# A LoRA, attention and FFN-adapter kernel: x is loaded and split at other places of a step, and the output projection runs one batch ahead of the conditioned weights

## The reference

```python
h = x @ W.T + b + 2.0 * ((x @ A[id]) @ Bm[id])      # LoRA projection, an adapter per batch
q, k, v = h @ w_q, h @ w_k, h @ w_v
o = softmax(q @ k.T / sqrt(32)) @ v                 # 32 heads, 8 key/value heads
x = x + o @ w_o
y = x @ cond2[id2].T                                # a 1024x1024 weight per batch
gates = softmax over the 2 largest of 4 of (y @ router_w.T)
x = x + 4.0 * sum_e gates_e * (y @ A_e.T) @ B_e.T   # rank 16, 4 experts
```

## Time and profile before

| what | us |
|---|---|
| median of 3 runs | 1071.86 (1070.69 to 1072.41) |
| profiled execution, its own time | 1075.97 |
| its span | 1074.3 |
| PE busy, of the span | 1018.2 (95%) |
| DVE busy | 635.1 (59%) |
| ACT busy | 450.3 (42%) |
| POOL busy | 233.7 (22%) |

### The profile page before, as it was taken

The page is one execution under the profiler, slowest core; times in us unless marked ns, Lnnn a source line. Parts: engine busy times, 40 slices in busy tenths (PEclk is TensorE's granted clock), DMA queues, the critical chain, the costliest instruction groups (busy, mean ns, idle before and its releaser), DMA issues.

```text
span 1074.3 us, 17421 instructions
## 1 busy us (share of the span) xinstructions
PE 1018.2 (95%) x6934; PEld 822.1 (77%) x6934; DVE 635.1 (59%) x1071; ACT 450.3 (42%) x782; POOL 233.7 (22%) x224
## 2 busy tenths in 40 slices
PE   7999999999899998999989999899799999999997
PEld 6878787877578775777767787577488898898896
DVE  6562734567755578654776557664555655655653
ACT  5121223355544466543664556544523323323320
POOL 1000001133223333223331236443200100100100
PEclk9999999999899998999998999899989999999998
DMA  7030312011421124211132125435757667667531
GB/s 257 0 99 18 111 55 72 22 36 37 116 57 37 35 53 115 58 34 31 45 97 71 44 81 153 115 115 175 225 165 233 210 189 230 213 184 231 196 118 40
DMA packets 49888, 117.41 MB, mean 109 GB/s; under 512 B 7298, under 2 KB 26114, under 8 KB 45712
## 3 DMA queue, kind: packets, MB, share of 16 engines
q1 hardware_dynamic: 40080, 81.70, 26.0%
q0 software_dynamic: 9728, 34.61, 10.1%
HBM read 86.38 MB, written 18.89 MB: 98 GB/s over the span
## 4 chain that ended last, share of the span: by engine, by line
PE 83%; DVE 6%; ACT 4%; DMA 4%; POOL 1%; SPq 1%; issue 1%; ACTq 0%
PE psP L752 17%; PE psW L1038 16%; PE psF L254 11%; PE psG L1066 8%; PE psO L820 5%; PE psT L807 4%; PE psS L796 4%; PE psP L767 3%; PE psX L1281 3%; PE psO L824 3%; DVE q_stack L652 2%; PE psY L1300 2%; ACT probs L599 2%; ACT q_stack L565 1%; PE psF L265 1%; PE psM L831 1%
## 5 line engine op out<-in xcount | busy, mean ns | idle before, releaser
L672 DVE TENSOR_REDUCE nmax<-psS 128x2 f32<-128x512 f32 x256 | 164.7, 685 | 178.5 <-PE psS L796 176.8
L549 POOL TENSOR_TENSOR p_sum<-probs 128x512 f32<-128x512 f32 x128 | 167.1, 1305 | 395.3 <-ACT probs L599 395.1
L752 PE MATMUL psP<-x_hl,wq 128*128 128x512 f32 x960 | 238.1, 393 | 3.7 <-DVE q_stack L652 3.7
L752 PEld LDWEIGHTS psP<-x_hl,wq 128*128 128x128 f32 x960 | 174.8, 189 | 35.7 <-issue 4.4
L1038 PE MATMUL psW<-wq 128*128 128x256 f32 x1536 | 197.4, 284 | 1.6 <-DVE q_stack L652 1.1
L1038 PEld LDWEIGHTS psW<-wq 128*128 128x128 f32 x1536 | 191.1, 191 | 6.3 <-issue 1.5
L599 ACT ACTIVATE probs<-psT 128x512 f32<-128x512 f32 x256 | 139.1, 595 | 46.9 <-PE psT L807 45.8
L1047 ACT ACTIVATE cond_hi<-cond_raw 128x1024 fp32r<-128x1024 f32 x64 | 66.8, 1057 | 154.3 <-PE psG L1066 149.9
L1051 DVE TENSOR_TENSOR cond_lo<-cond_raw,cond_hi 128x1024 fp32r<-128x1024 f32 x64 | 78.3, 1235 | 89.7 <-ACT cond_hi L1047 89.6
L614 ACT ACTIVATE nmax_rows<-psM 16x128 f32<-16x128 f32 x64 | 17.1, 268 | 190.5 <-PE psM L831 190.5
L652 DVE TENSOR_TENSOR q_stack<-psP,q_stack 32x512 fp32r<-32x512 f32 x128 | 87.8, 686 | 8.0 <-ACT q_stack L565 5.9
(11 more groups left out here) (122 smaller groups left out, 1261.8 us busy)
## 6 DMA issues: line engine op xcount, KB each, us to landing
cond_raw<-in_cond POOLq DMA_DIRECT2D x64, 512.0 KB, 4.0
x_raw<-in_xT SPq DMA_DIRECT2D x32, 256.0 KB, 4.0
q_stack<-q_stack SPq DMA_DIRECT2D x32, 256.0 KB, 3.1
o_scratch<-o_sb SPq DMA_DIRECT2D x64, 128.0 KB
o_raw<-rden_scratch SPq DMA_DIRECT2D x32, 256.0 KB, 5.3
o_raw<-o_scratch SPq DMA_DIRECT2D x8, 1024.0 KB, 9.4
x_sb<-in_xT SPq DMA_DIRECT2D x8, 1024.0 KB, 6.8
outT<-x_sb SPq DMA_DIRECT2D x32, 256.0 KB, 2.5
```

What stands on the lines that cost most here:

```text
L549: pool.tensor_tensor(p_sum[:, heads], probs[:, 0, heads], probs[:, 1, heads], ALU.add).then_inc(sum_done, 1)
L672: dve.tensor_reduce(nmax[:, n % 2, 2 * hp:2 * hp + 2, qt], psS[:, i % 2].rearrange("p (h k) -> p h k", h=2), AX.X, ALU.max, negate=True).t ...
L752: mm = pe.matmul(out, wq[:, i, w, k * P:(k + 1) * P], x[:, k, part], start=(k == 0 and n_ == 0), stop=False)
```

## The change

It does four things. (1) `WORK` is laid out anew: each q and k unit is split among other half steps; q1 lies wholly in the step before its pair, v0 in part 0 of s = 0 and v1 in part 1 of s = 1; (9, 1), (11, 1) and (12, 1) are empty; `project_u` is cut in two halves of four k-tiles. (2) The loads of x stand at the head of SP's steps 11 (k-tiles 0 to 5) and 12 (6, 7), where they stood at the end of 10, 11 and 12. ACT's hi parts are 0 to 5 in step 11, 6 and 7 in step 12. DVE's lo parts are 0 to 2 ahead of maxima 2 and 3 of step 12, 3 to 5 behind them, 6 and 7 in step 13; q7 is copied out behind them. (3) The output projection runs a batch ahead: batch 1's tiles 0 to 4 stand in steps 16 to 18 and its last three in `first()`; batch n then does the projection of n+1. x has three slots. The o and x of batch 1 are loaded at the end of step 12, o of batch 2 at step 17. (4) The last two batches share the last 8 tiles (`two()`), at which 16 rows are placed.

```diff
 WORK = [
...
-    (["q5:5-8"], ["q6:0-2"]),
-    (["q6:2-4"], ["q6:4-6"]),
+    (["q5:5-8"], ["q6:0-3"]),
+    (["q6:3-6"], []),
     (["q6:6-8"], ["q7:0-3"]),
-    (["q7:3-5"], ["q7:5-6"]),
+    (["q7:3-6"], []),
     (["q7:6-8"], []),
-    (["+u"], ["+k0:0-5"]),
-    (["+k0:5-8", "+q0:0-2"], ["+q0:2-8"]),
-    (["+q1:0-2"], ["+q1:2-4"]),
+    (["+u:0-4"], ["+u:4-8"]),
+    (["+k0"], ["+q0"]),
+    (["+q1:0-4"], ["+q1:4-8"]),
 ]
...
 def evacuated(n, part):
...
+    behind_x = [(p, u) for p, u in finished(n, 0) if u == "q7" and p + 1 < PAIRS]
+    if part:
+        return finished(n, 1) + behind_x
...
         def step(n):
+            if more:
+                for k in {11: range(0, 6), 12: range(6, KT)}.get(s, ()):
+                    load_x(sp, p + 1, k)
             if 1 <= n <= N:
...
-            if more:
-                for k in {10: range(0, 3), 11: range(3, 6), 12: range(6, KT)}.get(s, ()):
-                    load_x(sp, p + 1, k)
...
-                for k in {11: range(0, 3), 12: range(3, KT)}.get(s, ()):
+                for k in {11: range(0, 6), 12: range(6, KT)}.get(s, ()):
                     split_x_hi(act, p + 1, k)
...
+            if more:
+                for k in {12: range(0, 3), 13: range(6, KT)}.get(s, ()):
+                    split_x_lo(dve, p + 1, k)
...
+            if more and s == 12:
+                for k in range(3, 6):
+                    split_x_lo(dve, p + 1, k)
...
-    FIRST_TILES = {(12 + (m + 1) // 2, (m + 1) % 2): m for m in range(KT)}
+    TWO_AT = [[0, 1], [2, 3], [4, 5], [6, 7], [], [8, 9, 10], [11, 12, 13, 14, 15], []]
+    TWO_SPLIT = [[2, 3], [4, 5], [6, 7], [], [8, 9], [10, 11, 12], [13, 14, 15], []]
+    AHEAD = 5
+    FIRST_TILES = {(12 + (m + 1) // 2, (m + 1) % 2): divmod(m, KT) for m in range(KT + AHEAD)}
...
         if s == 12:
             sp.wait_ge(before.proj_done, PAIRS * NS)
+            load_o(sp, 1)
+            load_x(sp, 1)
             sp.dma_start(ra_raw[:], RA).then_inc(const_landed, 16)
-        if s == 13:
-            load_x(sp, 1)
-            load_o(sp, 1)
+        if s == 17:
+            load_o(sp, 2)
...
-        if part == 1 and s == 9:
-            normalise(dve, 0)
-        if part == 1 and s == 11:
-            scale_lo(dve, 0)
-        m = FIRST_TILES.get((s, 0) if part else (s - 1, 1))
-        if m is not None:
-            residual(dve, 0, m)
+        if part == 1 and s in (9, 13):
+            normalise(dve, (s - 9) // 4)
+        if part == 1 and s in (11, 15):
+            scale_lo(dve, (s - 11) // 4)
+        tile = FIRST_TILES.get((s, 0) if part else (s - 1, 1))
+        if tile is not None:
+            residual(dve, *tile)
...
+        def two():
+            n = B - 2
+            for m in range(KT):
+                w_o_tile(pe, n + 1, m, range(4))
+                if m == 4:
+                    turn_g(n)
+                if m == 7:
+                    y_tile(n + 1, 2)
+                    y_tile(n + 1, 3)
+                    turn_g(n + 1)
+                w_o_tile(pe, n + 1, m, range(4, KT))
+                if m == 4:
+                    middle(n)
+                for r in TWO_AT[m]:
+                    cond_row(pe, n + r // KT, r % KT)
+                if m == 1:
+                    turn_gated(n)
+                if m in (2, 3):
+                    y_tile(n, 2 * (m - 2))
+                    y_tile(n, 2 * (m - 2) + 1)
+                if m == 6:
+                    turn_gated(n + 1)
+                    y_tile(n + 1, 0)
+                    y_tile(n + 1, 1)
+            middle(n + 1)
```

More of the change, by code:

```diff
@@ L308, in work @@
 def work(n, part):
-    for w in FIRST.get(n, WORK[n % STEPS])[part] if n < N else []:
+    for w in WORK[n % STEPS][part] if n < N else []:
         p = n // STEPS + (w[0] == "+")
@@ L323, in evacuated @@
 def evacuated(n, part):
[L325 to L328, removed]
+    behind_x = [(p, u) for p, u in finished(n, 0) if u == "q7" and p + 1 < PAIRS]
+    if part:
+        return finished(n, 1) + behind_x
+    late = [(p, u) for p, u in finished(n - 1, 0) if u == "v0"] if n else []
+    return late + [(p, u) for p, u in finished(n, 0) if u != "v0" and (p, u) not in behind_x]
 def unit(p, u):
@@ L723, in free, with project_u @@
                 pe.wait_ge(before.tile_lo, CHUNKS * KT)
-        def project_u(p):
-            free(p, "u")
-            pe.wait_ge(a_lo_done, p + 1)
+        def project_u(p, first, end):
+            if first == 0:
+                free(p, "u")
+                pe.wait_ge(a_lo_done, p + 1)
             out = psP[0:64, bank(p, "u")]
-            for k in range(KT):
+            for k in range(first, end):
                 pe.wait_ge(x_lo_done, KT * p + k + 1)
@@ L772, in run_work @@
             for p, u, first, end in work(n, part):
-                if n == 0 and u == "q1":
-                    continue
                 if u == "u":
-                    project_u(p)
+                    project_u(p, first, end)
                 elif u[0] == "v":
@@ L908, in finish_stage @@
     const_landed, fb_landed = sem("const_landed"), sem("fb_landed")
[L909 removed]
+    o_landed, x_landed = ([sem(f"{v}_landed_{c}") for c in range(slots)] for v, slots in (("o", 2), ("x", 3)))
     o_normal, o_hi_done, o_lo_done = sem("o_normal"), sem("o_hi_done"), sem("o_lo_done")
@@ L1110, in ahead_tensor @@
     def ahead_tensor(pe, n, part):
-        m = FIRST_TILES.get((n - LAST, part))
-        if m is not None:
-            w_o_tile(pe, 0, m, range(KT))
+        tile = FIRST_TILES.get((n - LAST, part))
+        if tile is not None:
+            w_o_tile(pe, *tile, range(KT))
         k = ROWS_MULT.get((n - LAST, part))
@@ L1209, in add_y, with first @@
         def add_y(n, j):
-            c = (n - 1) % 2
+            out = x_sb[(n - 1) % 3][:, 2 * j:2 * j + 2]
             dve.wait_ge(y_done, YT * (n - 1) + j + 1)
-            dve.tensor_tensor(x_sb[:, c, 2 * j:2 * j + 2], x_sb[:, c, 2 * j:2 * j + 2],
-                              psY[:, j % 2].rearrange("p (m t) -> p m t", m=2), ALU.add).then_inc(y_added, 1)
+            dve.tensor_tensor(out, out, psY[:, j % 2].rearrange("p (m t) -> p m t", m=2), ALU.add).then_inc(y_added, 1)
+        def first():
+            for e in range(E):
+                ins = dve.memset(chosen[:, e:e + 1], e - 1.5)
+            for i in range(E - 1):
+                dve.memset(later[:, i, 0:i + 1], 0.0)
+                ins = dve.memset(later[:, i, i + 1:E], 1.0)
+            ins.then_inc(chain, 1)
+            residual(dve, 1, 4)
+            cond_row(6)
+            normalise(dve, 2)
+            residual(dve, 1, 5)
+            cond_row(7)
+            dve.wait_ge(fb_hi_done, 1)
+            dve.tensor_tensor(fb_stack[ER:P], fb_raw[ER:P], f(fb_stack[ER:P]), ALU.subtract).then_inc(fb_lo_done, 1)
+            residual(dve, 1, 6)
+            turn_copies(0)
+            residual(dve, 1, 7)
+            scale_lo(dve, 2)
+            before.invert(dve, PAIRS - 1)
+            for k in (0, 1):
+                cond_row(KT + k)
@@ L1252, in batch @@
-            if n + 1 < B:
-                cond_row(KT * (n + 1))
-                cond_row(KT * (n + 1) + 1)
-        for n in range(B):
+                if m == 1:
+                    gated_part(n)
+                if m in (2, 3):
+                    add_y(n, 2 * (m - 2))
+                    add_y(n, 2 * (m - 2) + 1)
+                if m == 3 and n + 2 < B:
+                    normalise(dve, n + 2)
+                if m == 6 and n + 2 < B:
+                    scale_lo(dve, n + 2)
+            for k in (0, 1):
+                cond_row(KT * (n + 1) + k)
@@ new lines, in two @@
+        def two():
+            n = B - 2
+            gates(n)
+            for m in range(KT):
+                if m == 4:
+                    turn_copies(n)
+                if m == 7:
+                    for j in range(YT):
+                        add_y(n + 1, j)
+                    turn_copies(n + 1)
+                residual(dve, n + 1, m)
+                if m == 1:
+                    gated_part(n)
+                for r in TWO_SPLIT[m]:
+                    cond_row(KT * n + r)
+                if m in (2, 3):
+                    add_y(n, 2 * (m - 2))
+                    add_y(n, 2 * (m - 2) + 1)
+                if m == 4:
+                    gates(n + 1)
+                if m == 6:
+                    gated_part(n + 1)
@@ L1257, in vector @@
+        first()
+        for n in range(1, B - 2):
             batch(n)
+        two()
         gates(B)
```

184 lines of the change are left out of this document (93 added, 91 removed).

## The result

The changed kernel takes 1097.55 us (median of 4, 1091.71 to 1098.85), the kernel before 1072.13. The ratio is 1.021, with an interval of 1.018 to 1.025. A second measurement beside e9 gave 1096.46 and 1.020 (1.016 to 1.024). I had forecast 1058.9, a gain of 13 us, and a range that ended at 1068.

The account below looks back on a forecast made before the run. PE was taken as the bound, with only 56 us of idle and its slow clock to win. Pairs 13.5, first pair 1.0, edit 3 3.5, less edit 4's 5.0, gave 13.0: 1071.9 to 1058.9, range 1047 to 1068.

Parts of the forecast that it names:

- edits 1 and 2 at s = 1: In the pairs' new layout, v1 waits for ACT's copy of v0: 1.25 us lost a pair.
- The boundary: From scores(12, 2) to scores(14, 0): 11.2 us instead of 16.1, with PE idle 1.95; gain 4.9 a pair.
- rival B: Idles ahead of scores(14, 0) and behind the x loads lower the clock, some 2.5 us a pair: 1066.4; chance 0.19.
- My bound of 3 us: A PE wait over 3 us costs about 2 more in clock; 1.95 ahead of scores(14, 0) leaves it full.
- The other waits of the pairs: Per pair: project_u meets no wait, rows behind x loads lose 0.85; exps and sums give back 1.2, q1 1.0.
- C: Rival: maxima rows of step 10 land 9.2 us after issue, PE waits 5.1 a pair: 1079; chance 0.08.
- D: Rival: splits of x come no earlier, loads being the limit; 4.9 falls to 0.4 a pair: 1072; chance 0.06.
- Edit 3: Where attention runs out, output projection a batch ahead: gain of 4.3 or 2.3 us, taken as 3.5.
- All three waits: Tile 3 of batch 0 waits 3.3 us behind normalise(1), tile 7 1.5 behind scale_lo(1), tile (1, 4) 2.95 behind row 4.
- Edit 4: Last two batches: rows 10, 13 and 15 wait 1.25 us each, y_tile(7, 0) 1.1; 5.0 lost in all.
- hidden waits: Rival: more waits hidden than forecast, at o of batch 1, rows beside x loads and last rows: about 1047; chance 0.22.

Follow-up runs that it names:

- e9: Changed kernel with q2 kept early, part 1 of s = 1 empty and v1, v2, v3 a half step later: 1079.8 us, 1.004 to the kernel before.
- e3: Changed kernel with q2 ending a half step later and v1, v2, v3 placed as before the change: 1075.4 us, 1.001 to the kernel before.
- e5: e3 with VectorE leaving out three of four lo parts of q7 in the first three pairs: 1064.6 us, 0.991 to the kernel before.
- e7: e6 with lo parts 5 to 7 of x made on GpSimd instead of VectorE: 1053.8 us, 0.981 to the kernel before.
- e1: Attention stage of the changed kernel with the last stage of the kernel before: 1091.5 us, 1.015 to the kernel before.
- e4: Changed kernel with the residual ahead of normalise and scale_lo on VectorE: 1089.4 us, 1.016 to the kernel before.
- e6: Attention stage of e3 with the last stage of the kernel before: 1067.9 us, 0.992 to the kernel before.
- e10: The changed kernel itself, timed again on the chip of e9: 1096.5 us, 1.020 to the kernel before.
- e8: Attention of e7 with the changed last stage, residual first as in e4 and row 4's split a step later: 1051.7 us, 0.980 to the kernel before.
- e2: Attention stage of the kernel before with the last stage of the changed kernel: 1082.8 us, 1.008 to the kernel before.

## Why the prediction was wrong, point by point

**The step that failed: edits 1 and 2 at s = 1.** I wrote that v1 waits 1.25 for the copy of v0, and it waits 1.23. But I let the copying out of q2 follow at once, as `copy_heads` stands behind v0 on ACT, and did not check what else `copy_q` waits for. It waits for the slot, the slot for scores that v1 holds up, and v2 is 3.71 late, in each of three pairs. v2 then runs at the lower clock for most of its length, 2.4 us. I had priced this place at 1.25 a pair, 3.75 in all. e3 puts it at 21 us, and e9, which leaves q2 where it is, at 17.

**The boundary and the clock behind scores(14, 0).** The wait was named, and 2.48 us came for 1.95, in two of three pairs. That the numbers are close is partly luck. From scores(12, 2) to scores(14, 0) I had 11.2 us, of which 8.2 were PE's; it took 12.1, 12.9 and 12.7, and in the second pair PE was at work or in small waits for 10.0. The term of VectorE that I had too small is the five lo parts of x. I took 0.72 for each, 3.6 in all, and they take 5.4 where the wait is 2.48 and 4.3 where it is 1.20. VectorE and GpSimd, first pair, then second:

```profile
284.30 1.28 DVE L434 TENSOR_TENSOR x_hl<-x_raw,x_hl 128x512 fp32r<-128x512 f32 x2
...
286.22 1.29 POOL L549 TENSOR_TENSOR p_sum<-probs 128x512 f32<-128x512 f32 x1 [4.19 <-ACT probs L599]
...
427.68 2.38 DVE L434 TENSOR_TENSOR x_hl<-x_raw,x_hl 128x512 fp32r<-128x512 f32 x2
...
428.17 1.35 POOL L549 TENSOR_TENSOR p_sum<-probs 128x512 f32<-128x512 f32 x1 [2.76 <-ACT probs L599]
```

A lo part takes 0.68 us. Five of the 32 take 1.77 or 1.78: they start up to 0.6 us after a sum of GpSimd has begun, and end 0.55 us after that sum has ended. In the first pair the sum comes only after lo parts 6 and 7. No run moved the sum alone, so that it holds VectorE up is read from the traces and not tested.

The term of the clock was mine too, as rival B, and I gave it 0.19 because the idle was below 3 us. It did fall in these two pairs: 2.3 and 2.2 us at k0 and 0.3 at the scores. e5 and e7 show that this goes with the wait, and so does the first pair, with 1.20 of idle and no drop. My bound of 3 us came from two rows, with idles of 1.9 and 3.4. It left out the idles of 2.05 and 2.18 around 690, which I had named in rival B and behind which the clock had fallen.

**The other waits of the pairs.** `project_u` has no wait above 0.40, as forecast. The rows behind the loads of x were 0.40, 0.53 and 0.76 late for 0.85. The waits for exps and sums in s = 9 and 11 are gone, and of q1's 3.7 us 0.6 are left. Rivals C and D did not occur.

**Edit 3.** All three waits came, and each behind the instruction named. The sizes: 4.28 for 3.3, since `normalise` of batch 1 started 10.8 us after the first issue of its loads and not 9.8; 1.26 for 1.5; 4.51 for 2.95, since row 4 took 6.0 us from POOL to ACT and not 4.0:

```profile
786.78 1.65 POOL L1012 DMA_DIRECT2D cond_raw<-in_cond  x3
```

```profile
792.82 1.06 ACT L1062 ACTIVATE cond_hi<-cond_raw 128x1024 fp32r<-128x1024 f32 x1 [6.42 <-DMA cond_raw<-in_cond]
```

The o of batch 2, which the change loads at step 17, was issued from 782.25; that the two disturb each other is likely from the DMA share of 0.99 in the window of 792, and was not tried. The clock fell behind both long waits (tiles of 5.48 and 5.49 for 3.04). `middle(0)` ends at 819.3; less the 20.1 us of tiles and the 14.7 inherited, that is 784.5, where before it was 780.8 and 1.8 behind. So the 3.5 us of gain became 1.9 of loss. Most of it is in the sizes above and in the clock, which took 4.9 us at the two tiles where I had 2.1 and perhaps 2.

**Edit 4.** Waits of 1.07, 1.07, 1.37 and 0.93 for 1.25, 1.25, 1.25 and 1.1:

```profile
1059.42 0.68 PE L1081 MATMUL psG<-cond_hi,ra_hi 128*68 128x512 f32 x2 [1.07 <-DVE cond_lo L1066]
...
1067.76 0.68 PE L1081 MATMUL psG<-cond_hi,ra_hi 128*68 128x512 f32 x2 [1.07 <-DVE cond_lo L1066]
...
1072.11 0.68 PE L1081 MATMUL psG<-cond_hi,ra_hi 128*68 128x512 f32 x2 [1.37 <-DVE cond_lo L1066]
1074.89 0.38 PE L1361 MATMUL psY<-gated_hi,fb_stack 128*128 128x256 f32 x1 [0.93 <-DVE gated_lo L1233]
```

That is 4.4 for 5.0. The third is not the wait for a split slot: the chain of waits leads from it to a load of the row by POOL (3.78 us).

**How the miss adds up.** The profiled execution was forecast at 1063.0 and took 1098.3, 35.3 more. By the turn of 60 it is 29.2 behind the forecast (14.7 late for 14.5 early). The place at s = 1 is 19.9 of these (23.7 against e3's trace, less 3.75), the clock at k0 and the scores 5.0, and the longer boundary 4.1. Edit 3 adds 5.4 and edit 4 gives 0.6 back. The forecast and the measured median lie 38.7 apart, because the profiled execution is 0.7 above its median and not 4.1, as I had carried over from before.

**The range.** Its lower side was given to hidden waits and its upper side to rival B alone. B came true in part together with an unlisted wait, and all rivals were worked out one at a time. A wait that I had not read could only lie on the slow side, since every named one was already counted, and the range had no room for one.

## What to carry to other kernels

When a unit is moved to an earlier half step, list every wait of the instructions that copy it out, the reuse of its destination slot too, and look at what stands ahead of the instruction that frees it; here a v unit put in front of two matmuls held up ACT, DVE and a bank in turn. An idle of PE should be priced with a chance of the slow clock behind it as soon as it is near an idle that has shown one. A mean duration (here 0.72 us for a lo part) should be opened up before it goes into a sum: it can hide one long instance among short ones. A residual or a split on which PE waits belongs ahead of an instruction that waits for a DMA.

## What the hardware showed that I had not expected

The granted clock can fall to its lower level of 1.2 GHz behind an idle of 2.48 us, and need not. The wait ahead of scores(14, 0) is 2.47 or 2.48 us at 19 places of the traces of the changed kernel, e1, e3, e4, e6, e9 and e10. Behind 17 of them k0 takes 6.6 to 8.0 us, and behind two it takes 5.63. One of these two is in e10:

```profile
435.10 1.01 PE L803 MATMUL psS<-k_stack,q_stack 96*128 96x256 f32 x4 [2.48 <-DVE nmax L672]
435.94 5.63 PE L761 MATMUL psP<-x_hl,wq 128*128 128x512 f32 x24
```

At the eleven places where the same wait is 1.21 us or less (one each in the changed kernel and e4, all in e5, e7 and e8) k0 always takes 5.6. In e7 a tile behind an idle of 2.25 us takes 4.46 us for 3.04. Before the change an idle of 1.87 us at row 6 was not followed by a drop.

A lo part of x on VectorE takes 0.68 us, and in the changed kernel 1.77 or 1.78 when a sum of GpSimd has begun 0.1 to 0.6 us before it. This 1.1 us for lo part 7 goes, in the changed kernel and in e4, with the difference between a wait of 1.20 and one of 2.48.

Executions of e3, e4, e6 and e9 scatter by 6 to 13 us, those of e7 and e8 by 5. But e2 and e10, with long waits as well, scatter by only 2 and 3, so the scatter does not simply follow the waits, and its cause is open.
